# Counting edges in a graph-network kernel: the destination one-hots are built on ScalarE instead of VectorE

## The reference

```python
edge_index = jnp.stack([src, dst])
x = _layernorm(x + _L0_gnn_ref(x, edge_index, edge_attr_16, ...))   # mean of x[src] by dst, plus the last edge's attributes
x = _layernorm(x + _L1_gnn_ref(x, edge_index, ...))                 # three attention layers over the same edges
x = _layernorm(x + _L2_gnn_ref(x, edge_index, ...))                 # mean of x[src] by dst again
x = _layernorm(x + _L3_gnn_ref(x, src, dst, edge_attr_8, ...))      # a message for each edge, summed by src
```

## Time and profile before

| | |
|---|---|
| median of 3 runs | 5185.09 us (5183.49 to 5191.42) |
| the profiled execution's own time | 5186.89 us |
| its span, first to last instruction | 5185.1 us |
| busy in the span: PE, PEld | 84%, 66% |
| busy in the span: DVE, ACT, POOL | 73%, 34%, 39% |
| mean granted TensorE clock | 0.912 |

### The profile page before, as it was taken

One profiled execution on the slowest core, in us unless ns is written; L12 is line 12 of the kernel. 1 busy time (PEld: TensorE's weight loads), 2 busy tenths in 40 slices (PEclk: granted clock), 3 DMA queues, 4 the chain that ended last, 5 costly groups with the idle time before them and its releaser, 6 DMA issues.

```text
span 5185.1 us, 117815 instructions
## 1 busy us (share of the span) xinstructions
PE 4338.7 (84%) x41609; PEld 3404.3 (66%) x41610; DVE 3795.9 (73%) x5814; ACT 1745.8 (34%) x3004; POOL 2008.5 (39%) x1717
## 2 busy tenths in 40 slices
PE   6999998888886977788489999579667888888886
PEld 3998888888885545344389999565444555555554
DVE  6988887877774028788466666456317999999998
ACT  0000000000000435788338777326222333333332
POOL 2888888885002017600000000000007666666663
PEclk6999999999997779999789999879668999999998
DMA  1000000000000000000000000000002111111113
GB/s 52 6 6 5 5 5 5 6 5 2 0 0 2 0 10 7 8 5 3 23 1 4 4 4 4 16 2 6 8 11 44 37 36 36 36 36 36 36 36 25
DMA packets 204304, 74.84 MB, mean 14 GB/s; under 512 B 169391, under 2 KB 189694, under 8 KB 204030
## 3 DMA queue, kind: packets, MB, share of 16 engines
q1 hardware_dynamic: 151710, 41.23, 3.6%
q0 software_dynamic: 52448, 31.60, 3.6%
HBM read 57.79 MB, written 14.88 MB: 14 GB/s over the span
## 4 chain that ended last, share of the span: by engine, by line
PE 52%; DVE 24%; issue 11%; POOL 3%; ACT 3%; DVEq 3%; DMA 2%; SPq 0%; ACTq 0%; POOLq 0%
PE ps L1201 51%; DVE adj L1159 8%; DVE scratch L861 5%; DVE adj L1151 4%; POOL by_src L512 3%; ACT scratch L651 2%; DVEq L859 1%; DVE adj L1164 1%; DVEq L338 1%; DVE scratch L1074 1%; DVE hwork L1049 0%; DMA r_dram<-adj 0%; DMA hwork<-gat_out_b 0%; DMA hwork<-gat_out_a 0%; DVE hwork L859 0%
## 5 line engine op out<-in xcount | busy, mean ns | idle before, releaser
L1201 PE MATMUL ps<-hwork,scratch 128*125 128x125 bf16 (+1 forms) x25750 | 1927.6, 236 | 102.6 <-DVE scratch L861 93.3
L1201 PEld LDWEIGHTS ps<-hwork,scratch 128*125 128x125 bf16 (+1 forms) x25750 | 1851.9, 151 | 172.1 <-DVE scratch L861 127.4
L512 POOL DMA_INDIRECT by_src<-work x782 | 1121.6, 1434 | 262.4 <-issue 224.3
L1074 DVE SCALAR_TENSOR_TENSOR scratch<-scratch,cols,adj 125x625 f32<-125x625 f32 x1125 | 939.9, 870 | 307.6 <-ACT scratch L651 289.8
L651 ACT ACTIVATE scratch<-work,cols 125x625 f32<-125x625 f32 x1125 | 965.0, 903 | 244.1 <-PE ps L1201 231.7
L541 POOL DMA_INDIRECT adj<-r_dram,adj x832 | 808.5, 972 | 493.9 <-DMA adj<-by_src 253.0
L861 DVE TENSOR_SCALAR scratch<-hwork,edge_ids 128x3125 bf16<-128x3125 uint16 x830 | 885.7, 1067 | 0.0
L1201 PEld LDWEIGHTS ps<-adj 128*125 128x125 f16 (+3 forms) x4320 | 386.4, 158 | 419.7 <-issue 381.5
L1201 PE MATMUL ps<-scratch,X 125*64 125x250 f32 (+3 forms) x3000 | 557.5, 458 | 113.2 <-DVE scratch L1074 99.8
L527 POOL IOTA adj<- 128x125 uint16 x1 | 0.2, 246 | 1635.1 <-DVEq L1123 1635.1
L1201 PE MATMUL ps<-work,adj 64*128 64x512 f32 x1664 | 470.6, 635 | 166.4 <-DVE adj L1151 122.1
(11 more groups left out here) (257 smaller groups left out, 2819.8 us busy)
## 6 DMA issues: line engine op xcount, KB each, us to landing
adj<-r_dram,adj POOLq DMA_INDIRECT x832
adj<-q_dram SPq DMA_DIRECT2D x416, 31.2 KB
by_src<-work POOLq DMA_INDIRECT x782
by_src<-adj SPq DMA_DIRECT2D x1, 4165.0 KB
adj<-by_src SPq DMA_DIRECT2D x104, 40.0 KB, 2.0
work<-in_rec SPq DMA_DIRECT2D x46, 85.0 KB, 1.9
gat_out_a<-hwork SPq DMA_DIRECT2D x5, 312.5 KB
hwork<-gat_out_a SPq DMA_DIRECT2D x1, 1562.5 KB
```

What stands on the lines that cost most here:

```text
L512: g.indirect_dma_start(by_src, bass.IndirectOffsetOnAxis(ap=pos_now[:, h, k:k + 1], axis=0), rec_in[:, h, k, :], None).then_inc(rec_sent[h ...
L1074: v.scalar_tensor_tensor(slots[:, j % SLOTS, :], slots[:, j % SLOTS, :], cols[:, 2, j, h:h + 1], adj3[:, j, ds(b * BW, BW)], ALU.add, ALU. ...
L1201: return t_.matmul(o_, l, r, start=start, stop=stop, skip_group_check=skip)
```

## The change

The two builds of `onehot_dst` leave VectorE's loop. ScalarE makes the same one-hot from the same `iota` slice in two steps: the square of destination minus iota, written as 32-bit floats to `off_sq`, and then `relu(1 - square)`, which is 1 where they are equal and 0 elsewhere. The second waits for the first by the new semaphore `off_ready`. `dst_f` holds the destinations as floats; VectorE makes it once, in the preparation. ScalarE now runs the inner loop too, so it reads the window's three table entries, waits for `oh_used` (the buffer's matmuls are done) and for `last_chain` (its update of `lastmax` is done), and TensorE waits for `ohd_built` beside `oh_ready` before a chunk. The counting of `last_chain` starts one higher. ScalarE's small copy with the load of its function table moves ahead of the loop.

```diff
+        dst_f = hflat[0:CH, 2100:2100 + NCH]
+        off_sq = hflat[0:CH, 2900:2900 + 2 * T].rearrange("p (c n) -> p c n", c=2)
...
+            a.copy(small[0:1, 60:61], ones[0:1, 0:1]).then_inc(table_loaded, 1)
+            act.wait_ge(table_loaded, 1)
...
             with act.Fori(0, NT) as w:
-
-                a.copy(small[0:1, 60:61], ones[0:1, 0:1]).then_inc(table_loaded, 1)
-                act.wait_ge(table_loaded, w + 1)
-
+                k0, k1, back = (tab_load(act, i, w) for i in range(3))
+                with act.Fori(k0, k1) as k:
...
+                    for c in range(PAIR):
+
+                        act.wait_ge(oh_used, k * PAIR + c + 1)
+                        act.wait_ge(last_chain, k * PAIR + w + c + 1)
+                        a.activation(off_sq[:, c, :], iota[:, ds(w * T, T)], ACT.Square, bias=dst_f[:, ds(g * PAIR + c, 1)], scale=-1.0).then_inc(off_ready, 1)
+                        act.wait_ge(off_ready, k * PAIR + c + 1)
+                        a.activation(onehot_dst[:, c, :], off_sq[:, c, :], ACT.Relu, bias=ones[:, 0:1], scale=-1.0).then_inc(ohd_built, 1)
                 act.wait_ge(adj_summed, w + 1)
...
             v.tensor_copy(edge_ids[:], ids_p).then_inc(ids_ready, 1)
+            v.tensor_copy(dst_f, ids_p[:, 1, :]).then_inc(ids_ready, 1)
...
                         dve.wait_ge(oh_used, k * PAIR + c + 1)
-                        v.tensor_scalar(onehot_dst[:, c, :], iota[:, ds(w * T, T)], edge_ids[:, 1, ds(g * PAIR + c, 1)],
-                                        None, ALU.is_equal).then_inc(ohd_built, 1)
...
-                        dve.wait_ge(last_chain, k * PAIR + w + c + 1)
+                        dve.wait_ge(last_chain, k * PAIR + w + c + 2)
...
                         pe.wait_ge(oh_ready, k * PAIR + c + 1)
+                        pe.wait_ge(ohd_built, k * PAIR + c + 1)
```

More of the change, by code:

```diff
@@ L224, in build_gnn @@
             sem("tabc_ready"), sem("tab_ps"), sem("tab_ready"))
-        oh_ready, oh_used, ohd_built, last_chain = sem("oh_ready"), sem("oh_used"), sem("ohd_built"), sem("last_chain")
+        oh_ready, oh_used, ohd_built, last_chain, off_ready = sem("oh_ready"), sem("oh_used"), sem("ohd_built"), sem("last_chain"), sem("off_ready")
         adj_summed, last_turned, last_col = sem("adj_summed"), sem("last_turned"), sem("last_col")
@@ L551, in _ @@
             act.wait_ge(srt["stored"], 48)
-            with act.Fori(0, NT) as w:
-                a.copy(small[0:1, 60:61], ones[0:1, 0:1]).then_inc(table_loaded, 1)
-                act.wait_ge(table_loaded, w + 1)
+            a.copy(small[0:1, 60:61], ones[0:1, 0:1]).then_inc(table_loaded, 1)
+            act.wait_ge(table_loaded, 1)
+            act.wait_ge(tab_ready, 1)
+            act.wait_ge(iotas, 2)
+            act.wait_ge(ids_ready, 2)
+            with act.Fori(0, NT) as w:
+                k0, k1, back = (tab_load(act, i, w) for i in range(3))
+                with act.Fori(k0, k1) as k:
+                    g = act.snap(nc.s_assert_within(k - back, 0, NG - 1, skip_runtime_bounds_check_because="a window's steps lie in 0 to NG"))
+                    for c in range(PAIR):
[4 more added lines that the diff above has]
+                        a.activation(onehot_dst[:, c, :], off_sq[:, c, :], ACT.Relu, bias=ones[:, 0:1], scale=-1.0).then_inc(ohd_built, 1)
                 act.wait_ge(adj_summed, w + 1)
@@ L848, in _ @@
             dve.sem_inc(oh_used, PAIR)
+            dve.sem_inc(last_chain, 1)
             with dve.Fori(0, NT) as w:
@@ L1266, in _ @@
                 mm(ps[0:T, 6, 0:4], zeros[:, 0:T], zeros[:, 0:4], False, True, True).then_inc(adj_summed, 1)
-                pe.wait_ge(last_chain, w + k1 * PAIR + 1)
+                pe.wait_ge(last_chain, w + k1 * PAIR + 2)
                 pe.wait_ge(last_col, w + 1)
```

## The result

The changed kernel takes **5096.5 us** in the median of three runs (5096.43 to 5097.53), against 5185.09 before: a ratio of 0.9827 with a 95% interval of 0.9804 to 0.9849. Its profiled execution took 5096.43 us with a span of 5094.7. The forecast was 5109, in a range of 5056 to 5185.

The account below looks back on a forecast made before the run. A buffer's fixed loop between TensorE and VectorE was taken to bound the counts at 3.28 us a group, falling to 3.05. Gains of 84 - 13 + 6 - 1 = 76 us gave 5109 us, range 5056 to 5185.

Parts of the forecast that it names:

- What bounds the kernel: Building of the counts: one buffer's way from TensorE to VectorE and back, 3.28 us a two-chunk group, not a busy engine.
- Loop 1: Source one-hots, TensorE to VectorE and back: without a register row and the destination build, 3.03 us a group.
- Loop 2: ScalarE's one-hot for `c = 0`, from buffer release through square and relu to matmuls: 3.04 us, between 2.86 and 3.20.
- Loop 3: VectorE's `lastmax` update waits for ScalarE's one-hot and delays the next source build: 3.05 us a group, the longest loop.
- Slow builds: Some 129 slow source builds lose their slack in the `lastmax` update's loop, 0.1 us each: 13 us lost.
- A window's start: First source build of each of 25 windows comes 0.25 us earlier: 6 us gained, with ScalarE's table reads beside its copy.
- How many groups: Of 415 groups in the counts, 365 gain 0.23 us each, leaving out two for each window: 84 us.
- The cast to `dst_f`: VectorE's chain in the preparation gets longer by 0.5 to 1.0 us; 1 us added.
- The sum: Whole kernel: 84 - 13 + 6 - 1 = 76 us off the profiled 5186.9 us, so a median of 5109 us.
- TensorE's bound at 2.94: Rival in the counts: TensorE's own pace sets the period at 2.94 us, total 5056 us; chance 0.14.
- The slower rival: ScalarE's path in the counts is longer than the old one: period 3.48 us, total 5258 us; chance 0.10.

Follow-up runs that it names:

- the run with an idle wait: Kernel with zero destination one-hots and no ScalarE builds, plus a second, already met TensorE wait before each chunk's matmuls: 3.130 us a group, 5133.4 us.
- the run with the spare build ahead: Changed kernel, with VectorE also building the destination one-hot into an unread tile ahead of the source build: 3.279 us a group, 5172.7 us.
- the run with the third step: Changed kernel with an extra relu on ScalarE between square and relu, changing no value: 3.347 us a group, 5208.7 us.
- the slowest kernel: Changed kernel with an unread destination build behind the source build, and VectorE waiting for it before the `lastmax` update: 3.845 us a group, 5371.8 us.

## Why the prediction was right

**What bounds the kernel.** Right. A fixed loop and not a busy engine set 3.28 us a group: the extra build ahead of the source build brings 3.279 back, the same build behind it costs nothing.

**Loop 1, sources: 3.03.** Mis-sized; it is about 2.94, by the run with an idle wait, and not longer than that by the run without destination one-hots. The term that failed is the register row with the wait, which I took over at 0.19. Ahead of the source build it takes 0.065 to 0.108 (first line, the changed kernel); ahead of a destination build the rows reach 0.206, before (second line) as in the run with the spare build ahead (third line):

```profile
L874 DVEq FUSED_REGOPS  x830: 65/84/108, 105.8 to 1533.2; - x166
...
L859 DVEq FUSED_REGOPS  x1245: 53/64/206, 105.2 to 1623.0; - x178
...
L875 DVEq FUSED_REGOPS  x1245: 53/64/206, 105.8 to 1625.5; - x178
```

**Loop 2, ScalarE: 3.04.** Right, and it is the longest way, 3.03 in the late groups. There the matmuls of `c = 0` start 0.144 us after the relu's end, eight times in ten 0.143 to 0.145, and 0.084 after the end of the source build, which needs only 0.055. In the run with the third step, where the relu ends 0.26 behind the source build, they start 0.145 after it as well, and TensorE's distance between starts ahead of `c = 0` is 0.468 there and not 0.134: the late groups took 0.33 of the 0.34. The steps were forecast at 0.40 and took 0.400 and 0.403. That the whole came out so near 3.04 is in part luck. The square starts 2.05 us after the matmuls and not 2.10 (1319.71, the matmuls of that buffer at 1317.66), and the passing between the steps is 0.03 (1319.71 + 0.40 to 1320.14) and not 0.10; but from the relu to the matmuls it is 0.144 and not 0.04. TensorE's row with the wait for `ohd_built` stands there, which I had put at nothing as hidden:

```profile
L1274 PEldq EVENT_SEMAPHORE  x830: 51/51/51, 106.5 to 1534.2; - x166
```

**Loop 3, the update behind ScalarE: 3.05.** The mechanism is there as forecast, at `c = 1`: VectorE's sequencer takes its wait for the relu at 1318.83, goes round the loop, and comes to the row for the next build of `c = 0` at 1319.42, 0.11 after `oh_used` was raised at 1319.31, so the build of 1319.56 starts some 0.08 late. But it was not the longest way, as I had taken it: by the 0.084 and 0.055 above, the source build still ends 0.03 earlier than it would have to. The idle time that the timeline shows ahead of the update of `c = 0` makes the source build of `c = 1` some 0.08 late, and costs nothing: the matmuls of `c = 1` start 0.057 after the last one of `c = 0`. Taking 0.43 off ScalarE's way, loops 2 and 3 both, gave 2.955.

**Slow builds: 13 us lost.** Too much. 55 of the 830 builds took over 1.15 us, against 141 before, and the first 13 windows, which have them, had means of 3.04 to 3.07 against about 3.03 in the others: some 0.02 on 256 groups, 5 us.

**A window's start: 6 us gained.** 9.2 were: 0.37 each and not 0.25, since the first build also lost its register rows. ScalarE's table reads did run beside its copy: in the window that begins at 356.6 the square is done by 356.67 and the relu by 357.10, 0.85 us before the sources at 357.95.

```profile
356.27 0.40 ACT L567 ACTIVATE hwork<-hwork 128x125 f32 x1 [0.80 <-issue]
...
356.70 0.40 ACT L569 ACTIVATE hwork<-hwork,ones 128x125 bf16<-128x125 f32 x1
356.91 1.04 DVE L874 TENSOR_SCALAR scratch<-hwork,edge_ids 128x3125 bf16<-128x3125 uint16 x1
```

**How many groups: 365.** The first two groups of all windows together gave 2.3 us (-9.3 and +7.0): TensorE, at half its clock (granted 0.50 from 358.10 to 360.70 us of the changed kernel), is behind there, and VectorE only starts earlier and waits longer. The others are 340. **The cast to `dst_f`: 1 us.** 0.5.

**The sum.** Forecast 84 - 13 + 6 - 1 = 76; measured 79.9 + 2.3 + 9.2 - 0.5 - 0.8 + 0.3 = 90.4. Of the 14 us between the two, about 8 are the slow builds, 3 the groups and 3 the window's start. That the mean of 3.046 meets the forecast of 3.05 is luck: 3.05 was meant for groups without slow builds, which took 3.03, and with the 13 us of slow builds it would have been 3.09.

**The rivals.** TensorE's bound at 2.94 is real and lies 40 us below the changed kernel: one reordering on ScalarE reaches it. The slower rival is real as well and near: 0.34 us more on ScalarE's way, less than one of its own steps, made the kernel slower than before.

## What to carry to other kernels

Where two engines hand two buffers back and forth, add up the way of one buffer, through every engine that has to release it, and compare it with each engine's work; an instruction moved off that way gains time until the next longest way takes over (here 0.25 of the 0.34 us by which the sources' way became shorter), and one that lies in an engine's idle time costs nothing (3.050 against 3.046). When work goes to an idle engine, start there whatever does not need the shared buffer before waiting for it: here that was worth another 39 us. And on VectorE a semaphore wait for the instruction just issued stopped the sequencer, which cost 0.8 us a group here, so put such a wait where that instruction is long done.

## What the runs showed of the hardware that was not expected

A wait on VectorE for its own last instruction cost far more than the instruction: 3.845 us a group with it and 3.050 with the wait a chunk later, for the same builds.

The source build has two durations before and after, about 1.03 and 1.24 us. In all nine kernels those over 1.15 us fall only while GpSimd issues its first 612 indirect DMAs: the last one starts at 967 us before (the last of these DMAs is issued at 1245) and at 1068 after (1090). Their number follows the rhythm and not the count of DMAs: 141 before, 55 after, 194 with the extra build ahead, 13 in the slowest kernel, 5 with the third step, 416 in the run with an idle wait on TensorE. In that one most groups of the stretch took 3.21 us, and the later ones 3.017. During all 55 of the changed kernel a DMA instruction of GpSimd starts 0.69 to 0.82 us after the build, which holds for 8 of the other 535 builds of that stretch; before, it is 122 of 141 and 1 of 495. What in the two instructions collides was not tried.
